# A second-layer selective scan: tile sums by accumulating transfers, y added by turning matmuls, three of eight blocks by diagonals

## What is computed

```python
xl = concatenate([flat, flat, flipped, flipped])      # 4 directions, 4 * 192 = 768 rows
delta = softplus(dt_r @ W_delta + b_delta)
def step(h, inps):                                     # one position t
    u_t, dt, B_t, C_t = inps
    h = exp(dt[:, :, None] * A) * h + (dt * u_t)[:, :, None] * B_t[:, None, :]
    y = einsum('bdn,bn->bd', h, C_t) + Dv * u_t        # sum over n = 16 states
y = y1 + y2 + flip(y3) + flip(y4)                      # the directions are added
```

## Time and profile before

| | us |
|---|---|
| median of three runs | 18644.4 (18640.06 to 18658.74) |
| profiled execution, its span | 18660.7 |
| the scan stage within that span | 7187 (from 9030 to 16217) |

### The profile page before, as it was taken

How to read it: one execution, slowest core, us unless ns; L and a number is a source line. 1 busy time by engine, 2 the same in 40 slices (tenths; PEclk the granted TensorE clock), 3 DMA queues, 4 the chain that set the end, 5 groups by cost and what they waited for, 6 DMA issues and landing times. The chain is left out here.

```text
span 18660.7 us, 271066 instructions
## 1 busy us (share of the span) xinstructions
PE 16820.2 (90%) x78344; PEld 10186.0 (55%) x78344; DVE 16050.6 (86%) x12158; ACT 15162.6 (81%) x24326; POOL 12567.1 (67%) x6247
## 2 busy tenths in 40 slices
PE   8799998899996798879899999999999999989798
PEld 3355554455552364455566666666666666547374
DVE  3799998899996486479899999999999999879698
ACT  7699996799992555557899999999999999845556
POOL 0099993599990474135799999999999999700101
PEclk9899998899997899999999999999999999999899
DMA  5788886788879677777433333333333333441313
GB/s 175 230 242 245 236 250 208 233 246 237 247 223 249 217 224 222 253 237 277 166 113 112 113 112 119 113 112 113 112 112 114 122 113 113 125 138 54 104 53 101
DMA packets 898273, 3166.02 MB, mean 170 GB/s; under 512 B 145638, under 2 KB 180170, under 8 KB 872140
## 3 DMA queue, kind: packets, MB, share of 16 engines
q1 hardware_dynamic: 817612, 3011.91, 51.1%
q10 hardware_dynamic: 79104, 136.10, 2.4%
HBM read 2342.21 MB, written 805.32 MB: 169 GB/s over the span
## 5 line engine op out<-in xcount | busy, mean ns | idle before, releaser
L1788 DVE TENSOR_TENSOR_SCAN l1s_h<-l1s_da,l1s_pd 128x1024 f32<-128x1024 f32 x3072 | 6778.1, 2268 | 241.5 <-PE l1s_pd L1720 163.4
L1831 ACT ACTIVATE l1s_dm<-l1s_dut,l1s_bt 128x384 f32<-128x384 f32 x7424 | 4056.8, 604 | 74.0 <-PE l1s_pd L1720 73.8
L1814 ACT ACTIVATE l1s_da<-l1s_dl,l1s_a 128x1024 f32<-128x1024 f32 x3072 | 3496.9, 1138 | 32.0 <-DVE l1s_h L1788 31.0
L1720 PE MATMUL l1s_pd<-l1s_id,l1s_dm 128*128 128x128 f32 x22272 | 2967.8, 274 | 36.4 <-DVE l1s_h L1788 33.9
L1720 PEld LDWEIGHTS l1s_pd<-l1s_id,l1s_dm 128*128 128x128 f32 x22272 | 2561.9, 142 | 487.7 <-issue 287.9
L1694 POOL TENSOR_TENSOR l1s_pb<-l1s_h,l1s_cc 128x1024 f32<-128x1024 f32 x1024 | 2517.8, 2459 | 95.0 <-DVE l1s_h L1788 83.4
L1698 POOL TENSOR_TENSOR l1s_pa<-l1s_sm,l1s_cc 128x1024 f32<-128x1024 f32 x1024 | 2433.1, 2376 | 0.0
L1731 PE MATMUL l1s_py<-l1s_pb,l1s_both 128*128 128x512 f32 x4096 | 2157.4, 609 | 197.1 <-POOL l1s_pb L1694 197.1
L1689 POOL TENSOR_TENSOR l1s_sm<-l1s_h 128x1024 f32<-128x1024 f32 x928 | 2203.5, 2374 | 122.8 <-DVE l1s_h L1788 122.6
L1731 PE MATMUL l1s_py<-l1s_pa,l1s_id 128*128 128x512 f32 x4096 | 2113.4, 598 | 0.3 <-POOL l1s_pa L1698 0.3
L2654 POOL TENSOR_TENSOR l0sf_pr<-l0sf_h,l0sf_cc 128x1024 f32<-128x1024 f32 x768 | 1813.8, 2380 | 71.1 <-DVE l0sf_h L2736 54.8
(11 more groups left out here) (318 smaller groups left out, 30375.1 us busy)
## 6 DMA issues: line engine op xcount, KB each, us to landing
l1s_cc<-crows SPq DMA_DIRECT2D x1024, 512.0 KB, 3.7
l0sf_cc<-l0crowsf SPq DMA_DIRECT2D x512, 512.0 KB, 5.5
l0sb_cc<-l0crowsb SPq DMA_DIRECT2D x512, 512.0 KB, 5.5
l0sf_cc<-l0crowsf SPq DMA_DIRECT2D x512, 256.0 KB, 7.1
l0sb_cc<-l0crowsb SPq DMA_DIRECT2D x512, 256.0 KB, 7.1
dls<-l1p_dl SPq DMA_DIRECT2D x192, 512.0 KB, 7.0
duts<-l1p_dut SPq DMA_DIRECT2D x64, 1536.0 KB, 5.9
l1s_dut<-duts SPq DMA_DIRECT2D x64, 1536.0 KB, 7.2
```

The source lines that it names most:

```text
L1720: mm = pe.transpose(pd[:, s % 2, blk * 128:blk * 128 + 128], dm[:, rnd % 2, blk, j * 128:j * 128 + 128], idt[:, :])
L1788: dve.tensor_tensor_scan(h[:, s % 4, :], da[:, j, :], pd[:, s % 2, :], 0.0, ALU.mult, ALU.add)\
L1814: act.activation(da[:, j, :], dl[:, half, j, :], ACT.Exp, scale=a[:, HT * half + j, n:n + 1])\
L1831: ins = act.activation(dm[:, rnd % 2, blk, :], dut[:, half, blk, :], ACT.Identity, scale=bt[:, half, blk, n:n + 1])
```

## The change

- **Tile sums.** POOL no longer adds the first two tiles, nor does DVE in three rounds. POOL issues a transfer from SBUF to SBUF that adds tile 1 to tile 0 in place (`accum_op`, one 512 KB transfer a round, on POOL's own queue). The product with C of that sum (`low`) is made one round later. `h` becomes three rings, of 4, 2 and 2 tiles, and DVE waits for the transfer before it overwrites tile 1 two rounds on.
- **y.** The products are written backwards by POOL in the backward half. PE adds them into `py` as eight accumulating 128x128 transposes for each product instead of two full matmuls, so `py` holds y turned. After the last round ACT copies it to `yo` (`hold`), PE turns it back (`back_b` adds the two 64-row halves on the way: 16 transposes; `back_a`: 8), and DVE's `finish` follows.
- **Diagonals.** Three of the eight blocks go by diagonals for all 16 states, five by scaling and transposing.
- The two semaphores of the sums are held for the whole program. The store covers 64 rows of the second tile instead of 128.

The diff of the engines' programs, cut to its core:

```diff
-    DIAGONAL = [n for n in range(N) if n % 2 == 0 or n % 4 == 3]
-    SUMS_ON_DVE = (6, 13, 25)
+    SCALED = 5
+    HALF_OF = (range(0, 3), range(3, SCALED))
+    STEP_BLOCKS = ((range(0, 1), range(1, 3), range(3, 5)), (range(0, 2), range(2, 4), range(4, 5)))
+    RINGS = (4, 2, 2)
...
+        def tile(rnd, j):
+            return h[j][:, rnd % RINGS[j], :]
...
             @block.gpsimd
+                def issue_sum(b, rnd):
+                    pool.wait_ge(scan, nth(b * STEPS + rnd * HT + 1))
+                    pool.sem_inc(begun, 1)
+                    pool.dma_start(tile(rnd, 0), tile(rnd, 1), accum_op=ALU.add).then_inc(s_sum[rnd % 2], 16)
+
+                def times_c(b, rnd, prods, source, used, made):
+                    way = slice(None, None, -1 if rnd >= N else 1)
+                    pool.wait_ge(used, nth(b * ROUNDS + rnd - 2))
+                    pool.tensor_tensor(prods[:, rnd % 2, way], source, cc[:, rnd % 4, :], ALU.mult).then_inc(made, 1)
...
                 def body(b, first, final):
                     for rnd in range(ROUNDS):
-                        if rnd not in SUMS_ON_DVE:
-                            pool.tensor_tensor(sm[:, rnd % 2, :], h[:, rnd * HT % 4, :], h[:, (rnd * HT + 1) % 4, :], ALU.add)\
...
+                        issue_sum(b, rnd)
+                        high(b, rnd)
+                        if not (first and rnd == 0):
+                            low(*((b, rnd - 1) if rnd else (b - 1, ROUNDS - 1)))
...
             @block.tensor
+                    pe.wait_ge(diagd, nth(b * N + (N - 1 if half else n)))
+                    for blk in range(SCALED, BLOCKS):
+                        pe.matmul(pd[:, s % 2, blk * 128:blk * 128 + 128], dut[:, half, blk, j * 128:j * 128 + 128],
+                                  bd[:, n, blk - SCALED, :], start=True, stop=True)
...
-                    mm = pe.matmul(target[:, hs], weights[:, :], row[:, hs], start=(rnd == 0), stop=(rnd == ROUNDS - 1))
+                    for blk in range(BLOCKS):
+                        mm = pe.matmul(target[:, blk * 128:blk * 128 + 128], prods[:, rnd % 2, blk * 128:blk * 128 + 128], idt[:, :],
+                                       start=(rnd == 0 and blk % 4 == 0), stop=(rnd == ROUNDS - 1), is_transpose=True,
+                                       skip_group_check=True)
...
+                def back_b(b):
+                    pe.wait_ge(heldb, nth(b))
+                    for blk in range(BLOCKS):
+                        for fold in range(2):
...
             @block.vector
                         if j == 0:
-                            dve.wait_ge(prodb, nth(b * ROUNDS + rnd - 2))
-                        else:
-                            dve.wait_ge(summed, nth(b * ROUNDS + rnd - 1))
+                            dve.wait_ge(proda, nth(b * ROUNDS + rnd - 4))
+                        if j == 1 and not (first and rnd < 2):
+                            dve.wait_ge(s_sum[rnd % 2], summed(*((b, rnd - 2) if rnd > 1 else (b - 1, rnd + ROUNDS - 2))))
+                        if j == 2:
+                            dve.wait_ge(prodb, nth(b * ROUNDS + rnd - 2))
...
-                        if rnd == 0 and j == 2 and not first:
-                            finish(b - 1, 1, yb, finb)
-                        if rnd == 1 and j == 1 and not first:
-                            finish(b - 1, 0, ya, fina)
+                        if rnd == 2 and j == 0 and not first:
+                            finish_b(b - 1)
+                        if rnd == 3 and j == 0 and not first:
+                            finish_a(b - 1)
...
             @block.scalar
+                            for blk in range(SCALED, BLOCKS):
+                                ins = act.activation(bd[:, n, blk - SCALED, :], idt[:, :], ACT.Identity,
+                                                     scale=bt[:, half, blk, n:n + 1])
...
+                def hold(b, j, done, held):
+                    act.wait_ge(done, nth(b * ROUNDS + ROUNDS - 1))
+                    act.wait_ge(s_y[j], b * 16 + 16)
+                    act.activation(yo[:, j * HW:j * HW + HW], py[:, j, :], ACT.Identity).then_inc(held, 1)
```

More of the change, by code:

```diff
@@ L1718, in turn @@
                         for blk in blocks:
-                            if not (blk == LAST and diagonal(n)):
-                                mm = pe.transpose(pd[:, s % 2, blk * 128:blk * 128 + 128],
-                                                  dm[:, rnd % 2, blk, j * 128:j * 128 + 128], idt[:, :])
+                            mm = pe.transpose(pd[:, s % 2, blk * 128:blk * 128 + 128],
+                                              dm[:, rnd % 2, blk, j * 128:j * 128 + 128], idt[:, :])
                     mm.then_inc(trd, 1)
[L1724 to L1730, removed]
-                    mm = pe.matmul(target[:, hs], weights[:, :], row[:, hs], start=(rnd == 0), stop=(rnd == ROUNDS - 1))
-                    if half == 1:
-                        mm.then_inc(done, 1)
@@ L1741, in body, with back_a @@
+                def back_a(b):
+                    pe.wait_ge(helda, nth(b))
+                    for blk in range(BLOCKS):
+                        mm = pe.matmul(py[:, 0, blk * 128:blk * 128 + 128], yo[:, blk * 128:blk * 128 + 128], idt[:, :],
+                                       start=(blk % 4 == 0), stop=True, is_transpose=True, skip_group_check=True)
+                    mm.then_inc(backa, 1)
                 def body(b, first, final):
@@ L1841, in body @@
                         m, v = b + (rnd + 1) // ROUNDS, (rnd + 1) % ROUNDS
-                        for j, blocks in enumerate((range(0, 3), range(3, 6), range(6, 8))):
+                        for j, blocks in enumerate(STEP_BLOCKS[v // N]):
                             decay(b, rnd * HT + j)
+                            if not first and (rnd, j) == (1, 1):
+                                hold(b - 1, 1, yb, heldb)
+                            if not first and (rnd, j) == (2, 2):
+                                hold(b - 1, 0, ya, helda)
                             if ahead:
                                 times_b(m, v, blocks)
-                times_b(0, 0, range(0, BLOCKS))
+                times_b(0, 0, range(0, SCALED))
                 images(act, body)
+                hold(IMAGES - 1, 1, yb, heldb)
+                hold(IMAGES - 1, 0, ya, helda)
 def l1_out_proj(nc, x0, ys, zs, w, x1):
@@ L3052 @@
     out = nc.dram_tensor("out", (IMAGES, C, HW), F32, kind="ExternalOutput").ap()
-    build(nc, aps.pop("x"), aps, out)
+    with nc.semaphore("sums0") as even, nc.semaphore("sums1") as odd:
+        build(nc, aps.pop("x"), aps, out, [even, odd])
     r = run_bass_kernel_spmd(nc, [{f"in_{name}": a for name, a in arrays.items()}], core_ids=[0])
```

164 lines of the change are left out of this document (88 added, 76 removed).

## The result

The changed kernel takes **18539.9 us**, the median of four runs (18522.8 to 18543.5), against 18651.4 (18640.1 to 18658.7) for the kernel before: a ratio of **0.9941, 95% interval 0.9929 to 0.9953**. It is 111 us faster, well outside the 0.2% that can be told from no change, but less than half of the 249 forecast. The profiled execution took 18543.5 us with a span of 18541.7.

What follows compares the result with a forecast made beforehand. ACT paces the kernel before, DVE after: 211.6 + 1.2 + 4.0 = 216.8 us an image, 6938 for 32. That is 249 off 7187, taking the median from 18644.4 to 18395 us; range 18310 to 18700, chance 0.82.

Steps and rivals of the forecast that it cites:

- The bound before, the bound after: Stage of the scans: ACT sets the pace before, 220.7 us an image; DVE is the new bound, 211.6 before waits.
- DVE's 216.8 us an image: DVE in the scan stage: 211.6 of work, 1.2 waiting for turning back, 4.0 at the loop's turn.
- POOL's issue: POOL's issuing of the adding transfer each round: taken as 1 us, bounded by 0.33 and 2.33.
- Turning back: PE turning y back before DVE's finishes: DVE waits 1.0 us, then 0.1 to 0.2, together 1.2 an image.
- The turn of the loop: DVE's wait for PE where the loop turns: 4.0 us an image, staying as before.
- the rival with a bound above 1.89: POOL becomes the bound if its issue costs over 1.89 us; 18845 us at 2.33; chance 0.14 slower, 0.07 between.
- Nothing won in the forward half: Forward rounds, ACT 6.53 against DVE 6.54 us, lose to mutual waits: 18497 us, chance 0.15, or 18631, chance 0.05.
- The clock: PE's clock in the stage: nothing charged for more transposes; rival of a clock at half, 22100 us, chance 0.03.
- The step that failed: Adding transfer lands in 3.7 to 11.1 us, hidden under limits of 10.7 (POOL) and 10.9 (DVE); C has 14 us.
- that rival: Sums land late: at a landing of 11.1 us POOL's period is 6.72, total 18575 us; chance 0.03.
- Two of the prediction's signs: In the stage's profile: DVE at least 97% busy, and the sum's landing at 4 to 8 us.
- The two that were to show a wrong mechanism: DVE's idle time before scans exceeding 300 us, or anything outside the stage moving by over 20 us.

Runs made afterwards that it cites:

- Undoing ACT's relief or POOL's: Changed kernel with loads in pieces, and seven scaled blocks and one diagonal (ACT), 18602.3 us, or POOL adding the tiles itself, 18754.4 us.
- one step later: Changed kernel with DVE's two finishes behind the second scan of rounds 2 and 3 instead of the first: 18510.1 us.
- the one with pieces: Changed kernel with image loads spread one piece a round over rounds 5 to 11 and 20 to 24, not two bursts: 18416.8 us.

## Why the prediction was right and wrong

- **The bound before, the bound after.** Right. Undoing ACT's relief or POOL's puts the stage back on that engine. By the expectations' sums and 4.0 for a loop's turn the stages would be 32 x (220 + 4) = 7168 and 32 x (223 + 4) = 7264; they are 7123 and 7282. In the changed kernel ACT is at 6447 busy, where the prediction said near 6300.
- **DVE's 216.8 us an image.** Right in its terms, once the burst is gone: 6939.6 / 32 = 216.9. Part of the closeness is luck: the waits before the finishes cost 0.3 an image more than taken, the loop's turn 0.6 less, and 0.4 are late sums that are left.
- **POOL's issue.** Taken as 1 us, measured 0.88; the rival with a bound above 1.89 never came near.
- **Turning back.** Taken as 1.0 us for the third tile and 0.1 to 0.2 for the other, measured 38.0 / 31 = 1.2 and 0.35; one step later three quarters of it are gone.
- **The turn of the loop.** It stayed, as said, at 107 to 109 us of the stage in both the changed kernel and the one with pieces, 3.4 an image where 4.0 was taken.
- **Nothing won in the forward half.** Refuted: no regular wait for ACT or PE stands there in the kernel with pieces, though the sums are within 0.01 us.
- **The clock.** It stays at 0.99 with 31 transposes of 49 passes. The Trainium skill (TensorE: Matmul & The Clock Gate, Part 4: PE-mode transpose) says that transposes don't bring the full clock. The stage as a whole can't tell, since 18 of its 49 passes are full matmuls; what disagrees is the earlier trace rows, where only transposes ran in the microseconds before the rise.
- **The step that failed** is the transfer: "it is hidden at nearly all of its range; the cover is that lag of a round", and for C "still has over two rounds, 14 us, for 3.7". The limits were nearly right: DVE waited 1.77 and POOL 1.47 for a landing of 12.1, so they lay at 10.3 and 10.6, where 10.9 and 10.7 were worked out. Two sizes were wrong. The sum's range ended at 11.1, from a C that landed alone, and it lands after up to 12.8 in a burst. And C was priced by its median of 3.7 though the earlier trace rows has 10.7 in a burst beside it; with the adding transfers under way it became 19.0, against a lead of 16.4 us (from its issue at 11288.1 to the end of the scan at 11304.5), more than the 14 that the prediction gave it. I had written that late sums come "only beside an image's loads" and then priced that rival as an average over all 1024 rounds, and gave it 0.03. It comes twice an image, costs some 3.8 us an image, 123 in all, and took almost half of the gain.
- **The signs.** Two of the prediction's signs pointed at it: DVE was busy for 96.2% and not 97, and landings left the 4 to 8. The two that were to show a wrong mechanism did not fire (237.7 us of idle time before scans against 300, 6 us outside the stage against 20), so they were set too wide for this loss.

## What to carry to other kernels

Work out the slack of a wait and hold the worst landing against it, in the rounds where the large loads run, not the median; a transfer that gets onto the path brings every burst beside it onto the path. Spreading loads cost nothing in either kernel here, but it paid only where someone waited for a transfer. More buffers at one wait can move the delay to a place where it costs more; here that was most likely PE, whose program has an addition of late data ahead of the work everyone needs.

## What the runs showed of the hardware

- An adding transfer of 512 KB within SBUF holds POOL for 0.88 us to issue and lands after 4.5 at best and 7.4 in the median, where C's, of the same size but from memory, took 3.7 before the change and 4.7 beside it.
- Transfers of different queues slow each other: with the adding ones under way C's median rose from 3.7 to 4.7, and its worst, behind 4 MB of loads, from 10.7 to 19.0. With the loads in ACT's queue the worst was 15.9, and the first fetch behind them took 10.6 at most.
- Behind two stalls of PE its granted clock is at 0.50: after it stood 4.77 us for a late product (above), and after 3.93 us on its own issue at a turn of the changed kernel's loop. Both times it worked on at the lower clock for about 6 us. So a stall of PE can cost more than its length. The windows at that turn:

```profile
11226.20:11230.20 4.00, 1.71 (x16) 1.47 (x14) 3.44 (x2) 3.32 (x6) 3.11 (x3) 1.00 0.77 181
11230.20:11232.20 2.00, 0.36 (x1) 0.37 (x2) 0.24 (x1) 2.00 (x4) 2.00 (x1) 0.69 0.88 174
11232.20:11236.20 4.00, 4.00 (x20) 4.00 (x20) 1.43 (x1) 3.23 (x7) 0.22 (x1) 0.50 0.42 141
11238.20:11242.20 4.00, 3.55 (x32) 3.32 (x31) 3.70 (x3) 4.00 (x7) 2.88 (x3) 1.00 0.70 132
```

The clock is at 1.00 up to the jump, at 0.50 for the four microseconds behind it, and back at 1.00 six microseconds on.
